# Layer 1's causal attention: a step's outputs and sums are copied out of PSUM one unit later, and its sums are inverted two or four units later

## The reference, cut to what matters

```python
q = x @ Wq; k = x @ Wk; v = x @ Wv          # 16 query heads, 4 key/value heads, rotary on q and k
scores = q @ k.T / sqrt(64)                 # causal
y = softmax(scores) @ v
x = layernorm(x + y @ Wo)
```

## Time and profile before

| what | value |
|---|---|
| median of 3 runs | 3548.32 us (3546.62 to 3554.97) |
| the profiled execution, its own time | 3562.32 us |
| span of its trace | 3560.5 us |
| granted PE clock, mean over the span | 0.877 |
| the stage `l1a`, first to last exponential | 1235 to 1721 us |
| in 1236 to 1725 us: PE busy | 399.39 us |
| in 1236 to 1725 us: ACT, POOL, DVE busy | 314.99, 311.75, 261.56 us |

### The profile page before, as it was taken

One profiled execution on the slowest core, in us unless ns is written; L12 is line 12 of the kernel. 1 busy time (PEld: TensorE's weight loads), 2 busy tenths in 40 slices (PEclk: granted clock), 3 DMA queues, 4 the chain that ended last, 5 costly groups with the idle time before them and its releaser, 6 DMA issues. The chain is left out here.

```text
span 3560.5 us, 41284 instructions
## 1 busy us (share of the span) xinstructions
PE 2658.6 (75%) x14234; PEld 1504.4 (42%) x14234; DVE 1768.2 (50%) x4802; ACT 1263.8 (35%) x2524; POOL 971.4 (27%) x738
## 2 busy tenths in 40 slices
PE   6888875786736688878756697877767888678696
PEld 3323325564513233333532564554532233446475
DVE  4576645344758555555235485234325766433413
ACT  4234441342411266666214001223213445345421
POOL 1145550235355466656223000001011001012100
PEclk9989997997967799999878698987887999789898
DMA  2221102500544311111012000110003121110122
GB/s 102 78 47 39 39 2 76 199 22 13 161 118 95 100 42 40 32 41 29 13 54 38 14 18 36 71 31 9 5 24 73 26 26 14 44 57 1 55 95 71
DMA packets 177133, 182.48 MB, mean 51 GB/s; under 512 B 55262, under 2 KB 143663, under 8 KB 176163
## 3 DMA queue, kind: packets, MB, share of 16 engines
q1 hardware_dynamic: 167523, 167.35, 16.4%
q0 software_dynamic: 9408, 12.56, 2.3%
HBM read 121.68 MB, written 61.59 MB: 51 GB/s over the span
## 5 line engine op out<-in xcount | busy, mean ns | idle before, releaser
L916 POOL TENSOR_TENSOR l1a_p_lo<-res,l1a_p_hi 128x1024 f16<-128x1024 f32 x192 | 311.8, 1643 | 180.0 <-ACT res L1157 180.0
L1166 ACT ACTIVATE l3a_probs<-ps 128x1024 f32<-128x1024 f32 (+1 forms) x192 | 148.8, 809 | 175.0 <-PE ps L1020 137.1
L1166 ACT ACTIVATE l0a_probs<-ps 128x1024 f32<-128x1024 f32 (+1 forms) x192 | 145.6, 810 | 179.2 <-PE ps L1020 104.7
L1156 ACT ACTIVATE l1a_p_hi<-ps 128x1024 f16<-128x1024 f32 x192 | 157.8, 822 | 112.0 <-PE ps L1020 82.6
L1017 PE MATMUL ps<-l1a_qs,l1a_ks 128*128 128x512 f16 (+3 forms) x768 | 167.5, 332 | 32.2 <-ACT res L1157 32.2
L986 PE MATMUL ps<-l1a_ks,l1a_qs 128*128 128x512 f16 (+3 forms) x384 | 121.6, 345 | 66.2 <-DVE l1a_nmax L1191 35.3
L1188 DVE CUSTOM_DVE_ANT_0 l1a_masked<-ps,l1a_wide_mask 128x128 bf16<-128x128 f32 (+3 forms) x256 | 118.0, 489 | 102.7 <-PE ps L986 100.4
L941 POOL TENSOR_TENSOR l0a_both<-l0a_probs 128x768 f32<-128x768 f32 (+2 forms) x96 | 154.6, 1633 | 47.1 <-PE ps L1058 46.9
L1157 ACT ACTIVATE res<-ps 128x1024 f32<-128x1024 f32 x192 | 158.1, 824 | 0.0
L1020 PE MATMUL ps<-mask_t,ident_b 128*128 128x128 bf16 x768 | 156.0, 224 | 0.0
L986 PE MATMUL ps<-l3a_ks,l3a_qs 126*128 126x512 f16 (+3 forms) x384 | 126.1, 363 | 38.1 <-DVE l3a_nmax L1188 22.1
(11 more groups left out here) (702 smaller groups left out, 6324.4 us busy)
## 6 DMA issues: line engine op xcount, KB each, us to landing
f_w<-in_L_ffn_w_dram SPq DMA_DIRECT2D x16, 1024.0 KB, 7.4
f_slots<-x0a_zeros SPq DMA_DIRECT2D x32, 256.0 KB, 4.8
f_xe<-f_slots SPq DMA_DIRECT2D x32, 256.0 KB, 3.2
f_ys<-f_y SPq DMA_DIRECT2D x32, 256.0 KB
l1a_qs<-l_q_h SPq DMA_DIRECT2D x64, 128.0 KB
d_wall<-in_L_ffn_W_dram SPq DMA_DIRECT2D x3, 2112.0 KB, 16.6
l0a_qs<-l_q_h SPq DMA_DIRECT2D x32, 128.0 KB
l0a_ks<-l_k_h SPq DMA_DIRECT2D x16, 256.0 KB
```

Of the source, the lines that this page charges most:

```text
L916: pool.tensor_tensor(ph_lo[:, n % SLOTS, :, 0:w], probs[:, n % FULL, :, 0:w], ph_hi[:, n % SLOTS, :, 0:w], ALU.subtract).then_inc(s_["low_ ...
L1156: act.activation(ph_hi[:, n % SLOTS, :, 0:w], SB[n % 2][:, :, 0:w], ACT.Exp)
L1166: act.activation(probs[0:KR, n % SLOTS, 2 * pr:2 * pr + 2, 0:w], SB[x % 2][:, :, 0:w], ACT.Exp).then_inc(s_["exps"], 1)
```

## The change

Two positions move, both for `split` only. On ACT, the copying out of step s - 1 stood between the exponentials of units 1 and 2 of step s, and stands between those of units 2 and 3 now. On DVE, the inversion of step s stood behind all items of step s + 1 (its last unit). Now it stands behind the items of unit 3 of step s + 2 if that step is long, of unit 1 if it is short. No instruction is added or removed, and PE, POOL and SP keep their own order.

```diff
-    invert_after = [[s for s in range(S) if s + INV < S and plan.first_unit[s + INV + 1] - 1 == n] for n in range(U)]
+    turn_over = LAG + 1
+    at_unit = [plan.first_unit[s + 2] + (3 if len(steps[s + 2].units) > 2 * GQ - 1 else 1) if split and s + 2 < S else plan.first_unit[s + INV + 1] - 1 if s + INV < S and not split else U for s in range(S)]
+    invert_after = [[s for s in range(S) if at_unit[s] == n] for n in range(U)]
...
-                        if n - plan.first_unit[s] == LAG and s:
+                        if n - plan.first_unit[s] == turn_over and s:
                             evacuate(s - 1)
...
-                for s in range(max(S - INV, 0), S):
-                    invert(s)
+                for s in range(S):
+                    if at_unit[s] == U:
+                        invert(s)
```

## The result

The changed kernel took 3586.93 us (median of 5 runs, 3579.32 to 3598.85), the kernel before 3554.97 us (5 runs, 3546.62 to 3561.55). The ratio is 1.0094, with a 95% interval of 1.0065 to 1.0122. It is slower by about 0.9%, some 33 us, where I had forecast 3551 us and no change.

The account below looks back on a forecast made before the run. PE was taken as nearest to its limit, 25.0 of 30.8 us a pair. 14 pairs x (0.5 - 0.1) = +5.6, ends -2.5, together +3 us on 3548.3: 3551 us (own range 3543 to 3559; over cases 3506 to 3562).

Parts of the forecast that it names:

- Copying out, long step: ACT and PE in a long step: unit 4's scores start 3.3 us earlier, a gross gain of 1.8 + 1.4 + 0.1 us.
- the 1.41 us: PE's wait before the scores of unit 4 in a long step, put down to the copying out; forecast to go.
- the 2.32: PE's 2.32 us wait before a long step's third plain maximum, put down to DVE standing in the inversion.
- the hold: DVE's inversion instructions wait for POOL's running subtraction to end (shared port); forecast to give back 3.0 to 3.2 us a long step.
- that rival: The hold is not met in the new places: a long step gains 3.0 us, -43 in all, 3505 us; chance 0.15.
- The inversion in its new place: DVE in the long step: add slips in at POOL's boundary, third and fourth instructions wait, PE's next item starts at 1439.6.
- A long step gains 0.1 us: the hold gives back 3.0 to 3.2 of the 3.3: Net forecast for a long step: the 3.3 us gained earlier, nearly all lost while PE's program queues behind the inversion.
- Short step: 0.55 us before unit 0's scores go, but the inversion delays the turn: a loss of 0.25 or 0.8 us, taken as 0.5.
- SP: SP's queue: loads and the long step's sums come 6 us later, at no cost.
- The cover: Time between the sums landing (1463.1) and the long step's inversion wanting them (1466.0): 2.9 us; without it the old wait returns.
- The sum: 14 pairs x (0.5 - 0.1) = +5.6 us, stage ends -2.5, together +3 us.
- The slower one: Rival: the short step's third instruction is also held, turn 1.05 us late, +11, 3559 us; chance 0.17, including any unseen loss.

Follow-up runs that it names:

- The seventh experiment: The changed kernel with the long steps' inversions back at their old place, the short steps' kept in the new one: 3629.26 us, ratio 1.0197 to the kernel before.
- the third: The changed kernel with POOL subtracting only 8 columns in units 3, 4 and 5 of long steps: 3519.11 us, ratio 0.9885 to the kernel before.
- the fourth: The changed kernel with 20 zero-operand matmuls on PE where it waits in the long step: 3561.43 us, ratio 1.0008 to the kernel before.
- the sixth: The changed kernel with the short steps' inversions back at their old place, the long steps' in the new one: 3567.99 us, ratio 1.0021 to the kernel before.
- the second: The kernel before with only the inversions moved, the copying out left between units 1 and 2: 3596.3 us, ratio 1.0098 to the kernel before.

## Why the prediction was wrong, step by step

- **Copying out, long step: right.** ACT's wait of 75.9 us is 2.5, the 1.41 us are gone and 0.57 are left of the 2.32, and where the hold is taken away a pair falls to 28.3 us, near the 27.9 (30.8 - 3.0 + 0.1) of that rival.
- **The inversion in its new place: the wait right, its price wrong.** I had the add slip in at one of POOL's boundaries, the third and fourth instructions held, and PE's item at 1439.6, behind one that ended at 1439.25 - 3.3 = 1435.95 (1438.71 + 0.54, less the gain): a wait of 3.65 us, which my last paragraph calls "about 3". The add passed (0.16 us), the third and fourth were held 1.79 and 1.55 us, to the ends of POOL's subtractions, and PE waited 3.59. With the clock held up the pair is 31.3 us against my 31.2.
- **The step that failed** is "A long step gains 0.1 us: the hold gives back 3.0 to 3.2 of the 3.3". I priced the hold by the time that it takes from PE's schedule, and gave the matmuls behind it the durations of the earlier trace rows, which are those of a clock of 1.00. But the change gathers most of PE's idle time, 2.32 + 1.41 + 0.45 us in three places, into one wait of 3.59. Behind the single waits of before the clock stayed at 1.00 in 11 of 14 pairs. Behind the gathered one it fell in all 14, and the same matmuls took 2.8 us longer a pair. The term that the sum lacked is this one: +2.8 us a pair for the clock. The rows at 0.95 in the earlier trace rows, with PE busy for 26.6 us instead of 25.0, had shown that the clock can fall in this stage and what that costs, and I used them only to compare two pairs.
- **Short step: the mechanism right, the size at the upper end.** The fourth instruction was held (0.67 us) and the turn waits 1.24. Less the 0.55 before unit 0's scores, which went as forecast, that is 0.7, where I took 0.5 from 0.25 or 0.8.
- **SP: right.** The cover held: of the 14 waits for `y_col` none is left in the pairs; the one of 3.8 us stands at 1755 us, in the stage's end. The seventh experiment shows what is behind it when it isn't there.
- **The sum.** 14 x 0.4 - 2.5 = +3 us. PE's idle time in the stage rose by 6.3; of the 3 us that I missed there, 14 x 0.2 are the short step's. The 27.7 us of longer matmuls had no term. By pairs, 14 x 2.8 = 39 would be the clock's price; the stage shows less, because two of the pairs run at 0.95 and three pairs of the kernel before already did. The sum of +3 us is a ratio of 1.0008, and the kernel with 20 zero matmuls came out at just that; to the last digit this is luck, since its interval is 0.9989 to 1.0026.
- **Rivals.** The slower one was on the right side for the wrong reason: it asked for 1.05 us at the turn and would have made +11. Its chance took in "any loss that I haven't seen", but no rival of mine had the clock in it, and the range ended at 3562.

Shown by experiment: the hold makes the wait (the third), and the clock behind the wait makes the loss (the fourth: DVE as late as ever, some 30 of the 33 us gone). Left open: what, beside the wait's length, decides whether and how far the clock falls. A 2.0 us wait lets it fall in four pairs of 14; a 3.6 us wait leaves pairs at 0.90, at 0.95 or, once, at 1.00, and it costs less with the short steps' inversions at their old place (the sixth) or with the copying out at its own (the second).

## What to carry to other kernels

A wait on TensorE has two prices, its own length and the clock of the matmuls behind it: a change that gathers several short waits into one long one can lose with the total idle time nearly unchanged (here 96.0 and 102.3 us). To see it, split a stage's growth into busy and idle time of PE before looking for a new wait. And before an instruction is moved away from a late input, ask why the input is late: here the reordering of nine loads on SP's queue won 69 us together with half of this change, and 27 by itself, where this change lost 33.

## What the runs showed of the hardware

- After 3.59 us without work PE's granted clock was 0.54 over the next 6.6 us, and a pair of L1040's matmuls took 0.64 us instead of 0.38. It came to 2.8 us of a 34.1 us pair.
- After waits of 1.98 and 1.99 us the clock of the next 6.7 us was 0.75 in one pair and 1.00 in its neighbour (pairs of 32.9 and 31.3 us). After waits of 2.32 us it was 0.74 and 1.00 over 6.6 us. With a wait of 3.63 us one pair in 14 kept 1.00.
- Twenty matmuls whose moving operand is all zeros, in a wait of 3.6 us, kept the granted clock at 1.00 and made the changed kernel some 30 us faster.
- A DVE instruction of 8 columns that takes 0.17 us alone took 1.79 and the next 1.55 us beside POOL's back-to-back subtractions, of which three take 5.81: each is held to the end of one of them, and one gets in at each boundary. With POOL's subtractions cut to 8 columns both took 0.17. The add just ahead of them, 0.16, was not held.
